# Products that nobody reads, issued on TensorE in three lulls of a two-layer decoder kernel

## The reference

```
x = x + causal_attention(layernorm(x))        # 16 heads of 8, rotary positions      (A0)
x = x + cross_attention(layernorm(x), ctx)    # 16 heads, 77 context tokens          (X0)
x = x + experts(layernorm(x))                 # 8 experts, each token uses its top 2 (M0)
x = x + full_attention(layernorm(x))          # 16 heads of 8                        (A1)
x = x + one_head_cross_attention(...)         #                                      (X1)
x = x + quantised_conv_mlp(layernorm(x))      #                                      (F1)
```

## Time and profile before

| what | value |
|---|---|
| three runs | 790.69, 795.36, 798.61 us, median 795.36 us |
| profiled execution | 790.39 us, span on the core 788.6 us |
| TensorE busy (matmuls) | 642.6 us, 81% of the span |
| VectorE, ScalarE, GpSimd busy | 568.7, 431.5, 282.6 us |
| mean granted TensorE clock | 0.908 |
| chain that ended last | TensorE 56%, VectorE 23%, issue 9%, GpSimd 5%, ScalarE 4%, DMA 2% |

### The profile page before, as it was taken

How to read it: one execution, slowest core, us unless ns; L and a number is a source line. 1 busy time by engine, 2 the same in 40 slices (tenths; PEclk the granted TensorE clock), 3 DMA queues, 4 the chain that set the end, 5 groups by cost and what they waited for, 6 DMA issues and landing times.

```text
span 788.6 us, 16027 instructions
## 1 busy us (share of the span) xinstructions
PE 642.6 (81%) x5006; PEld 348.9 (44%) x5011; DVE 568.7 (72%) x1685; ACT 431.5 (55%) x825; POOL 282.6 (36%) x512
## 2 busy tenths in 40 slices
PE   5679998989887884099999635597999989997987
PEld 2334454544344443099999612122232323234543
DVE  6877687787557766567777447788898898943574
ACT  1415665656665551055555321285887777884544
POOL 6654444555533157513333301224241340341310
PEclk9968999999999986589999856599999999999999
DMA  7744573451243211211111135212222111000000
GB/s 224 260 173 133 168 219 114 136 188 57 74 118 105 65 62 45 71 39 49 49 49 49 33 116 176 80 28 86 78 95 69 54 41 42 2 2 1 14 14 28
DMA packets 72803, 67.18 MB, mean 85 GB/s; under 512 B 14560, under 2 KB 67232, under 8 KB 72720
## 3 DMA queue, kind: packets, MB, share of 16 engines
q1 hardware_dynamic: 69488, 60.42, 24.9%
q0 software_dynamic: 2272, 4.69, 1.9%
q10 hardware_dynamic: 960, 1.05, 0.4%
HBM read 37.74 MB, written 28.00 MB: 83 GB/s over the span
## 4 chain that ended last, share of the span: by engine, by line
PE 56%; DVE 23%; issue 9%; POOL 5%; ACT 4%; DMA 2%; SPq 0%; DVEq 0%; POOLq 0%; ACTq 0%
DVE mx L600 12%; PE bank_pv L748 10%; PE bank_turn L584 7%; PE bank_scores L2069 5%; PE bank_turn L1803 5%; PE bank_scores L1803 4%; PE bank_scores L1811 4%; PE bank_scores L700 4%; POOL routed_tokens L1767 2%; PE bank_turn L767 2%; DVE xn L476 2%; DVE stats L455 2%; PE bank_turn L588 1%; PE bank_turn L809 1%; PE bank_turn L533 1%
## 5 line engine op out<-in xcount | busy, mean ns | idle before, releaser
L600 DVE TENSOR_REDUCE mx<-bank_turn 128x1 f32<-128x512 f32 (+3 forms) x452 | 259.6, 615 | 54.6 <-PE bank_turn L588 28.9
L584 PE MATMUL bank_turn<-stk 64*128 64x77 bf16 (+4 forms) x708 | 155.6, 305 | 34.3 <-DVE mx L600 23.4
L700 PE MATMUL bank_scores<-stk 64*128 64x512 bf16 (+3 forms) x576 | 171.6, 360 | 4.9 <-ACT probs L721 3.6
L725 ACT ACTIVATE probs<-bank_scores 128x1024 f32<-128x1024 f32 (+4 forms) x160 | 116.9, 769 | 93.1 <-PE bank_scores L700 92.0
L721 ACT ACTIVATE probs<-bank_scores 128x512 f32<-128x512 f32 x256 | 138.6, 606 | 35.4 <-PE bank_scores L700 34.4
L748 PE MATMUL bank_pv<-probs,vsl 128*32 128x512 f32 (+3 forms) x1152 | 138.6, 554 | 2.9 <-POOL probs L733 1.8
L584 PEld LDWEIGHTS bank_turn<-stk 64*128 64x128 bf16 x708 | 52.3, 97 | 137.8 <-DVE mx L600 67.0
L733 POOL TENSOR_SCALAR_AFFINE_SELECT probs<-probs 128x256 f32<-128x256 f32 x128 | 51.5, 407 | 71.4 <-ACT probs L725 69.8
L1783 POOL DMA_INDIRECT expert_outputs<-probs,y_at x39 | 37.3, 958 | 82.6 <-DVE y_at L1680 78.3
L482 POOL TENSOR_TENSOR rstd<-var,mhalf 128x4 f32<-128x4 f32 x24 | 24.6, 1024 | 108.1 <-DVE var L461 107.9
L700 PEld LDWEIGHTS bank_scores<-stk 64*128 64x128 bf16 x576 | 45.6, 94 | 29.8 <-ACT probs L721 17.6
(11 more groups left out here) (300 smaller groups left out, 1080.0 us busy)
## 6 DMA issues: line engine op xcount, KB each, us to landing
stk<-stack_A SPq DMA_DIRECT2D x64, 256.0 KB, 3.1
w<-in_M_w SPq DMA_DIRECT2D x12, 512.0 KB, 4.7
stack_A<-parts SPq DMA_DIRECT2D x11, 384.0 KB, 2.8
stack_A<-fill SPq DMA_DIRECT2D x8, 512.0 KB, 5.3
stk<-stack_X SPq DMA_DIRECT2D x16, 256.0 KB, 2.7
stack_A<-parts SPq DMA_DIRECT2D x11, 256.0 KB, 3.1
probs<-routed_tokens SPq DMA_DIRECT2D x39, 65.0 KB, 1.8
w<-expert_outputs SPq DMA_DIRECT2D x4, 512.0 KB, 5.8
```

The costliest lines, as they stand in the source:

```text
L584: mm = e.matmul(o, stk[r, slot, 0, pp, qt * P:(qt + 1) * P], stk[r, slot, 1, pp, 0:keys], start=True, stop=not a.causal)
L600: e.tensor_reduce(o.rearrange("p h q -> p q h"), bank_of((g, m))[:, 0:k * keys].rearrange("p (q h k) -> p q h k", q=len(tiles), h=len(hs)) ...
L700: mm = e.matmul(score_bank(g, kt, i)[:, 0:S - q0], stk[r, slot, 1, pp, kt * P:(kt + 1) * P], stk[r, slot, 0, pp, q0:S], start=True, stop=True)
L725: e.activation(probs[0:a.kp, probs_of(g, kt), j:HG:2, 0:n], bank_scores[0:a.kp, 2 * j:2 * j + 2, 0:n], ACT.Exp, scale=1 / math.sqrt(HD)).t ...
```

## The change

A helper `unread(e, n)` issues n matmuls of a constant (128 x 128 ones in bfloat16) by another constant (128 x 512, also ones) into `bank_st[3]`. They wait for nothing and raise no semaphore, and nothing reads the bank before a later matmul overwrites it. The helper is called in five places, 92 products in all: 12 before the turn of unit 0 (behind two waits, on the filled constant and on VectorE's reading of the last projection), one after each of the 12 maxima of unit 1, 20 before the first expert tile, 24 between the projections of batch 0 and 1 in the second attention layer, and one after each of the 16 maxima of unit 32 and the first 8 of unit 33.

```diff
+        def unread(e, n):
+
+            for _ in range(n):
+                e.matmul(bank_st[SINGLES], onesb[:], fill[:, 1], start=True, stop=True)
+
         def all_maxima_pe(e, g):
             for k in range(len(layer(g).items)):
                 max_pe(e, g, k)
+                unread(e, 1)
...
             for k in range(AHEAD, len(A0.items)):
                 max_pe(e, 0, k)
+            e.wait_ge(s_fill, 1)
+            e.wait_ge(s["up_dve"], 4 * NB)
+            unread(e, 12)
             turn_pe(e, 0)
             all_maxima_pe(e, 1)
...
             norm_pe(e, A1.ln, 0)
             stage1_pe(e, 0)
+            unread(e, 24)
             norm_pe(e, A1.ln, 1)
             stage1_pe(e, 1)
             all_maxima_pe(e, 32)
...
             for k in range(len(A1.items) // 2):
                 max_pe(e, 33, k)
+                unread(e, 1)
...
             e.wait_ge(s_experts, 16 * W_PIECES)
+            unread(e, 20)
             for t in range(2):
                 turn(t)
```

## The result

| kernel | median us | runs (lowest to highest) | ratio to before, 95% interval |
|---|---|---|---|
| before | 793.92 | 12 (788.58 to 798.61) | |
| the change | 802.4 | 12 (794.92 to 810.71) | 1.0108 [1.0075, 1.0141] |
| the change, second series | 803.92 | 4 (795.35 to 810.65) | 1.0104 [1.0014, 1.0193] |

The ratios are of the faster executions alone, without those over 1.5% above the fastest of their kernel; medians and ranges take in all. The forecast was 790.0 us in 783.5 to 797.5. The change costs 8.5 us by the medians instead of giving 3.0. The rival that ended on the other side, TensorE as the bound among unit 1's maxima at half clock, is what happened, and it happened again where I had put a net of nothing, in the second attention layer.

What follows compares the result with a forecast made beforehand. TensorE held 56% of the chain, with about 18% of the span at half clock. Gains of 1.3 (launch), 1.7 (experts), 0 and 0 sum to 3.0 us, from 793.0 to 790.0 us; range 783.5 to 797.5.

Steps and rivals of the forecast that it cites:

- The rival that ended on the other side: Launch: half clock makes TensorE the bound among unit 1's maxima, 4.8 us later, 797.8 us; chance 0.10.
- Launch, 12 products: Before unit 0's turn: they fill a 4.07 us lull, turn moves -0.1 to +0.4 us, taken as 0.
- Launch, unit 1's maxima: One product per maximum fits under VectorE's pace at full clock: 1.3 us gained, bounds 0 to 2.2 us.
- The price: Each added product: 0.22 us at full clock, 0.43 at half, with 0.38 and 0.60 as other ends.
- Experts, 20 products: Before the first expert tile: clock kept, first 16 expert products take 1.95 instead of 3.62 us, 1.7 us gained.
- Second layer, 24 products: Between batch 0's and 1's projections: clock falls again in a 3.2 us lull, 0 us; up to 1.9 if kept.
- Second layer, 16 + 8 products: Unit 32's cost nothing, unit 33's lose about 1 us, clock rises near 508: net 0, bounds -1.8 to +2.0 gain.

Runs made afterwards that it cites:

- the blocks alone: The change without its 36 single products beside the maxima, keeping the rows of 12, 20 and 24: 788.0 us, ratio 0.9961 to the kernel before.
- the block alone: The change with only the 20 products ahead of the first expert tile, all other added products taken out: 789.59 us, ratio 0.9965 to the kernel before.
- the singles alone: The change with only the 36 single products beside the maxima, the rows of 12, 20 and 24 left out: 810.2 us, ratio 1.022 to the kernel before.

## Why the prediction was wrong, step by step

- **"Launch, 12 products": right, 0.** In both profiles of the change they ran at full clock and were over 1.38 us before the turn, which moved by what had moved ahead of it. Where the clock fell inside the block, as with the blocks alone, they took the 4.4 us that I had as the worst case, and the turn moved by 0.2 us.
- **"Launch, unit 1's maxima": wrong, and the step that failed.** It said that 12 products add 2.6 us and that "5.6 us still fit" in 6.3, at full clock. Two things failed in it. The clock: I took it as held because 12 products went ahead "without a pause", but at 0.22 us each those 12 could not fill the 4.07 us lull, 12 x 0.22 = 2.6 us, and my own bound for that step only had them too long, never too short. Behind the pause the clock fell at about 55 us. I had also tied a fall to idle time behind the last product; with the blocks alone it came 1.0 us into the row of twelve, with TensorE busy, behind unit 0's maxima and their gaps. The price: 0.22 and 0.43 us are those of products in a row; beside a 64-row maximum a product took 0.32 and 0.54 us, between those and the 0.38 and 0.60 us I had kept as the other ends. So what I had as covered by VectorE's pace, a maximum and its product within 0.53 us, was 1.08 to 1.19 us of TensorE's own. Forecast 1.3 us gained, measured 6.7 us lost. The rival on the other side had the mechanism, and its 4.8 us were the 0.43 us again; its chance of 0.10 leaned on the missing pause.
- **"Experts, 20 products": right.** 1.7 us forecast, 1.2 us in the change and 1.3 us with the block alone; the first 16 products took 1.96 us as forecast. The idle times were shorter than forecast, 0.19 us ahead of the first transposition and 0.96 behind it instead of 1.0 and 2.0, inside what the clock had survived before.
- **"Second layer, 24 products": right about the clock, 0.9 us gained instead of 0.** The clock fell at 485 us, just as the projections began, so that only the transpositions ahead of them ran at full (0.66 us for four where unit 33's batch took 1.12), which is 0.45 us. The other 0.4 lies ahead of them and isn't the block's: the blocks alone had none of it, and the singles alone, without the 24, had 0.35.
- **"Second layer, 16 + 8 products": wrong.** Unit 33's eight did start at half, at 0.54 us and not 0.43, and the clock did not rise near 508: 4.0 us lost, with no gain behind. The rows spoke against that rise: TensorE is 100% busy at half for 6.5 us in 507.5 to 514.0 and for 7.4 us at the launch, so being busy had not brought the clock back there either. What had brought it back, at the experts, was products in a row. Unit 32's sixteen cost 0.6 us in one profile of the change and 6.9 us in the other; no term of mine had that. I took the clock as full there, and the trace of before speaks against it as well: among unit 32's maxima it falls at about 490 us, and is at half until 514; the mean of the stretch, columns as in the earlier trace rows, is 0.73.

```profile
484.00:497.00 13.00, 7.88 (x22) 1.80 (x20) 9.97 (x17) 1.40 (x3) 0.92 (x3) 0.73 0.15 51
```

My stretches left out 483.2 to 496.8 us, and with them the place where sixteen products were to go.

- **Still open:** why the clock fell among unit 32's pairs in some executions and held in others, and inside the block at the launch in some and not in others. The Trainium skill ("TensorE: Matmul & The Clock Gate", Part 1, note on the warm-up; this is also the page that the prediction calls the same page) says that the number of slow products differs between runs of one kernel, and the spread agrees, but no run here shows what decides. Nor was the 3.1 us behind unit 33 traced to an instruction; 2 us of it lie within what kernels with the same code differ by.

## What to carry to other kernels

Fill lulls, not the spaces between instructions that another engine paces: a product in a lull delays nothing if it ends before the work it warms for, and one between paced instructions makes TensorE the bound as soon as the clock falls, with nothing to bring it back. Size such a block at full clock, so that it reaches the next real work without a pause, and count what it costs if the clock falls inside it (18 products held the turn up by 1.5 us); price a product by its neighbours, not by a row of its own kind. Where an added instruction is safe at one clock and not at the other, the sum is two cases, and the case with the loss deserves the chance that the trace of before gives to the clock's falling there.

## What the runs showed of the hardware

- TensorE 100% busy stayed at half clock for 20 us (55.0 to 75.3 us of the change), while the same stretch stayed full with three products per maximum, also 100% busy, and, nearly as busy, with one where no pause stood ahead. Busy time on the profile doesn't say whether the clock will rise.
- Alternating with 64-row products of 512 columns, a 128-row product took 0.32 us at full clock and 0.54 us at half, against 0.22 us in a row of its own kind at full clock (14.62 us for the 66 recorded of 68).
- Real numbers and ones gave the same clock in the same places (unit 33's pairs at half with both; a block of 12 at the launch partly at half with both, 4.47 and 4.40 us).
- The clock fell while TensorE was issuing products in a row: at about 49.3 us with the blocks alone, 1.0 us into the twelve, behind maxima with gaps of 0.15 to 0.62 us.
- One kernel kept the clock among unit 32's maxima in one execution (17.01 us to the turn) and lost it in another (23.32 us).
- The stretch in which TensorE reads ten words took 7.01 to 7.07 us in three profiles, where VectorE showed 5.08 us.
